# A post-LayerNorm attention and FFN block on one core: the order of the banded mix within a group of tokens

## What is computed

```python
# x: (4, 512, 1024); w1, w2: (1024, 1024)
attn = jnp.einsum('ds,td->st', w1, w2) * sparse_mask      # three stripes: a band beside the diagonal
y = jnp.einsum('bds,st->bdt', x, attn) + b2
x = _layernorm(x + gelu(y, approximate=False))
# w_l: dense (1024, 1024) weights, decoded from 4 bit planes and a 16-entry table per row
y = einsum('bsi,oi->bso', x, w_l) + bias                  # 8-bit weights where a row's norm is over 64
x = _layernorm(x + y)
```

## Time and profile before

| what | before |
|---|---|
| median of three runs | 306.03 us |
| the profiled execution | 305.57 us |
| its span | 303.8 us |
| PE busy | 289.7 us (95%) |
| DVE busy | 197.4 us (65%) |
| ACT busy | 184.7 us (61%) |
| POOL busy | 112.8 us (37%) |
| mean granted TensorE clock | 0.989 |

### The profile page before, as it was taken

How to read it: one execution, slowest core, us unless ns; L and a number is a source line. 1 busy time by engine, 2 the same in 40 slices (tenths; PEclk the granted TensorE clock), 3 DMA queues, 4 the chain that set the end, 5 groups by cost and what they waited for, 6 DMA issues and landing times.

```text
span 303.8 us, 5068 instructions
## 1 busy us (share of the span) xinstructions
PE 289.7 (95%) x1907; PEld 254.7 (84%) x1907; DVE 197.4 (65%) x352; ACT 184.7 (61%) x245; POOL 112.8 (37%) x178
## 2 busy tenths in 40 slices
PE   8999898999999999999999999999999999999980
PEld 4788766666769999999999999999998887888880
DVE  2679988997868977898776786504135445344362
ACT  1966558988998967976986979251144452312210
POOL 4000003343344988898788600000033333322321
PEclk9999999999999999999999999999999999999995
DMA  6999999999999301111110111119237785443222
GB/s 225 398 355 356 378 383 288 252 262 224 206 190 199 89 19 37 35 37 35 37 41 32 52 55 35 54 36 245 103 131 257 239 272 203 169 167 140 105 120 97
DMA packets 28480, 49.77 MB, mean 164 GB/s; under 512 B 2464, under 2 KB 11936, under 8 KB 28448
## 3 DMA queue, kind: packets, MB, share of 16 engines
q1 hardware_dynamic: 23392, 40.53, 39.1%
q0 software_dynamic: 4352, 8.39, 15.4%
q10 hardware_dynamic: 704, 0.46, 0.5%
HBM read 36.79 MB, written 12.58 MB: 163 GB/s over the span
## 4 chain that ended last, share of the span: by engine, by line
PE 80%; SPq 7%; DVE 4%; DMA 3%; ACT 2%; issue 2%; POOL 0%; DVEq 0%; ACTq 0%
PE acc L560 20%; PE acc L562 20%; PE acc L561 20%; PE acc L543 5%; PE acc L489 4%; DMA w<-in_w2d 3%; PE acc L464 2%; SPq L275 2%; PE acc L499 2%; PE acc L465 2%; PE acc L466 2%; SPq L279 1%; SPq L274 1%; PE acc L431 1%; PE acc L476 1%
## 5 line engine op out<-in xcount | busy, mean ns | idle before, releaser
L560 PE MATMUL acc<-lin,zz 128*128 128x256 f32 (+2 forms) x424 | 130.2, 307 | 0.3 <-issue 0.3
L562 PE MATMUL acc<-lin,zz 128*128 128x256 f32 (+2 forms) x424 | 129.8, 306 | 0.0
L561 PE MATMUL acc<-lin,zz 128*128 128x256 f32 (+2 forms) x424 | 129.6, 306 | 0.0
L560 PEld LDWEIGHTS acc<-lin,zz 128*128 128x128 f32 x424 | 80.0, 189 | 4.6 <-issue 0.5
L561 PEld LDWEIGHTS acc<-lin,zz 128*128 128x128 f32 x424 | 80.2, 189 | 4.0
L562 PEld LDWEIGHTS acc<-lin,zz 128*128 128x128 f32 x424 | 80.1, 189 | 4.1
L725 ACT ACTIVATE leaf<-planes,lut,flip 128x1024 f32<-128x1024 uint8 x56 | 67.4, 1238 | 1.3 <-DVE dest L999 1.3
L999 DVE COPY_PREDICATED leaf<-planes,leaf 128x1024 f32<-128x1024 uint8 x32 | 43.6, 1362 | 12.6 <-ACT leaf L725 11.8
L1394 POOL DMA_DIRECT2D z<-in_xr x16 | 19.5, 1220 | 70.9 <-ACT z L707 69.4
L828 ACT ACTIVATE junk<-rows,cols 128x1024 bf16<-128x1024 f32 x15 | 17.2, 1150 | 39.6 <-POOL cols L1368 39.6
L1366 POOL TENSOR_TENSOR cols<-cols 128x1 f32<-128x1 f32 x15 | 9.0, 603 | 74.6 <-DVE rows L1119 74.6
(11 more groups left out here) (110 smaller groups left out, 438.3 us busy)
## 6 DMA issues: line engine op xcount, KB each, us to landing
z<-in_xt SPq DMA_DIRECT2D x16, 512.0 KB, 9.4
z<-in_xr POOLq DMA_DIRECT2D x16, 512.0 KB, 8.7
out_rows<-rows SPq DMA_DIRECT2D x15, 512.0 KB, 2.9
out_rows<-parts SPq DMA_DIRECT2D x32, 128.0 KB, 1.7
rows<-out_rows SPq DMA_DIRECT2D x16, 256.0 KB, 2.7
w<-in_w1d SPq DMA_DIRECT2D x7, 512.0 KB, 9.2
off_band<-in_mask_rest SPq DMA_DIRECT2D x8, 448.0 KB, 4.4
w<-in_w2d SPq DMA_DIRECT2D x3, 584.0 KB, 9.0
```

The lines of the kernel that those rows point to most:

```text
L560: nc.tensor.matmul(bank, hi, w_hi, start=k == 0, stop=False)
L561: nc.tensor.matmul(bank, hi, w_lo, start=False, stop=False)
L562: last = nc.tensor.matmul(bank, lo, w_hi, start=False, stop=k == KB - 1)
```

## The change

In each group, TensorE now takes own products of units 0 to 3, then pairs 2, 0 and 1 with excess 0 between pair 2 and pair 0, then own products of units 4 to 7, then excess 1, pairs 5 and 3, excess 2, and pairs 4 and 6. Before, it was own 0 to 3, excess 0, pairs 0, 2; own 4 to 6, excess 1, pairs 1, 3, 5; own 7, excess 2, pairs 4, 6. ScalarE's and VectorE's lists follow the new order in which units are finished, and `MIX_STEPS` deals one decode step of group 0 and one of group 1 differently. The count of instructions of every kind in the mix is the same.

```diff
-    MIX_STEPS = [(3, 3), (2, 1), (2, 1), (2, 0)]
+    MIX_STEPS = [(3, 2), (3, 1), (2, 1), (2, 0)]
...
-    BESIDE = (0, 2, 1, 3, 5, 4, 6)
+    BESIDE = (2, 0, 1, 5, 3, 4, 6)
...
+                beside(g, 2)
                 excess(g, 0)
                 beside(g, 0)
-                beside(g, 2)
-                for t in (4, 5, 6):
+                beside(g, 1)
+                for t in (4, 5, 6, 7):
                     own(g, t)
-                excess(g, 1)
-                beside(g, 1)
-                beside(g, 3)
-                beside(g, 5)
-                own(g, 7)
                 if g == FIRST_TURN_GROUP:
                     pe.wait_ge(consts_made, 4)
                     turn(0)
+                excess(g, 1)
+                beside(g, 5)
+                beside(g, 3)
                 excess(g, 2)
                 beside(g, 4)
                 beside(g, 6)
...
                 gelu(g, 0)
-                done = decode_steps(MIX_STEPS[g][0], done)
+                if g == FIRST_TURN_GROUP:
+                    done = decode_steps(MIX_STEPS[g][0], done)
+                gelu(g, 1)
+                gelu(g, 2)
+                if g != FIRST_TURN_GROUP:
+                    done = decode_steps(MIX_STEPS[g][0], done)
+                for pair in MIX_Z.get(g, ()):
+                    make_z_hi(*pair)
+                if g == FIRST_TURN_GROUP:
+                    make_lin_hi(0)
                 if g + 1 < GROUPS:
                     make_xe_hi(g + 1)
-                gelu(g, 1)
-                if g + 1 < GROUPS:
                     make_x_hi(g + 1, 1)
-                if g == FIRST_TURN_GROUP:
-                    make_lin_hi(0)
-                gelu(g, 2)
-                gelu(g, 3)
-                for pair in MIX_Z.get(g, ()):
-                    make_z_hi(*pair)
-                done = decode_steps(MIX_STEPS[g][1], done)
-                gelu(g, 4)
-                gelu(g, 5)
+                for t in (3, 4, 5):
+                    gelu(g, t)
                 if g + 1 < GROUPS:
                     make_x_hi(g + 1, 3)
                 gelu(g, 6)
                 if g + 1 == GROUPS:
                     make_lin_hi(1)
                 gelu(g, 7)
+                done = decode_steps(MIX_STEPS[g][1], done)
...
-                done = decode_steps(MIX_STEPS[g][0], done)
+                if g == FIRST_TURN_GROUP:
+                    done = decode_steps(MIX_STEPS[g][0], done)
                 if g + 1 < GROUPS:
-                    make_xe_lo(g + 1)
                     make_x_lo(g + 1, 0)
-                    make_x_lo(g + 1, 1)
+                if g != FIRST_TURN_GROUP:
+                    done = decode_steps(MIX_STEPS[g][0], done)
                 for pair in MIX_Z.get(g, ()):
                     make_z_lo(*pair)
                 if g == FIRST_TURN_GROUP:
                     make_lin_lo(0)
-                if g != GROUPS - 2:
-                    done = decode_steps(MIX_STEPS[g][1], done)
                 if g + 1 < GROUPS:
+                    make_x_lo(g + 1, 1)
+                    make_xe_lo(g + 1)
                     make_x_lo(g + 1, 2)
                     make_x_lo(g + 1, 3)
                 else:
                     make_lin_lo(1)
-                if g == GROUPS - 2:
-                    done = decode_steps(MIX_STEPS[g][1], done)
+                done = decode_steps(MIX_STEPS[g][1], done)
```

## The result

| what | before | after |
|---|---|---|
| median of 22 runs each | 305.81 us | 306.56 us |
| ratio, after to before | | 1.0022, 95% interval 1.0014 to 1.0029 |
| the profiled execution | 305.57 us | 306.93 us |
| its span | 303.8 us | 305.1 us |

The change makes the kernel slower by 0.22%, some 0.7 us. The forecast was 306.1 us, 0.1 us over the 306.03 us that were known of the kernel before. Four of the 22 executions of after took 310.7 to 312.6 us, none of before did; the ratio leaves them out, and the last experiment shows in a trace what such an execution can be.

What follows compares the result with a forecast made beforehand. The mix was taken to end at a gate that ScalarE and VectorE open, so PE's gains are given back: -0.02 us by the walk, +0.1 for hand-overs, on the median 306.1 us; range 305.3 to 307.1.

Steps and rivals of the forecast that it cites:

- likeliest case: Whole kernel: the forecast of 306.1 us, with its own range from 305.5 to 306.6 us; chance 0.61.
- slower: Whole kernel: a time over 306.6 us, slower by more than 0.2%; chance 0.24.
- Rival B: PE's waits for itself cost more than a hand-over from another engine: 0.9 us more, 307.0 us; chance 0.20.
- Part 1, mode changes: PE in each group: four array mode changes instead of six, at 0.21 us each, save 0.42 us.
- Part 2, PE's waits for itself: Per group, pair 1 waiting for pair 0 adds 0.35 us, pair 4 waiting for pair 3 adds 0.12 us.
- Part 3, group 0: turn(0) waits some 1.6 us for gelu 1, starting at 47.62; group 1 starts at 52.25, before 52.48.
- Part 4: Groups 1 and 2: 12.30 us per group against 12.25 without a stall; group 1's old 0.6 us wait goes.
- Part 5, ScalarE's chain and the gate: Group 3: new 0.76 us stall for x_lo at own product 2; linear product at 93.69 us, before 93.71.
- Covers: Group 0's excess 0 loses its 0.47 us xe wait without gain; loads of x and xe have many microseconds of slack.
- A: PE's waits for itself cost nothing in the mix: 1.1 us less, 305.0 us; chance 0.15.
- C: Clock falls to 1.2 GHz in the new wait ahead of turn(0) in group 0: 310.5 us; chance 0.04.

Runs made afterwards that it cites:

- the last experiment: Changed kernel with gelu 1 of group 0 ahead of the third leaf and one group 3 leaf behind the last gelu: 305.49 to 312.09 us, traced execution 310.96 us.
- the first experiment: Changed kernel plus one needless wait per group, pair 3 also waiting for pair 5 right ahead of it: 307.68 us, ratio to before 1.0064.

## Why the prediction was right, and where it was not

The range held, and the likeliest case by a hair: 306.56 us, in 305.3 to 307.1, with "slower" from 306.6 on. Some of this is luck. The forecast was a change of 0.1 us on a base of 306.03; the change is 0.7 us, and the base, by 22 runs, 305.81. So the number was better than the reasoning, and what was missing is the mechanism of Rival B. By its own parts:

- **Part 1, mode changes.** The changed kernel shows them at the same size: 52.65 (the last of pair 6) to 52.97 and 0.34 to the next. The 0.42 us per group were saved: 12.25 - 0.42 and 0.68 of the waits below make 12.51, and a group took 12.55.
- **Part 2, PE's waits for itself: the step that failed.** Both terms were put too low, 0.35 for 0.45 us and 0.12 for 0.23. Pair 1 comes 0.57 us behind pair 0's last matmul (42.30 to 42.87) and 0.34 more to the next: 0.45 over two spacings of 0.23, where I had 0.35. Pair 4: 0.35 and 0.34, so 0.23, where I had 0.12. The modelled end was a good end (42.30 + 0.39 = 42.69); it was the hand-over from there that is 0.18 and not the 0.10 that I had carried over from VectorE to PE. In groups 1 and 2 this is 2 x 0.21 = 0.42 of the 0.51 us that were missing. A group has 0.68 us of such waits against 0.42 of mode changes saved: the exchange loses. The one more wait of the first experiment, 0.4 us per group, says the same.
- **Part 3, group 0.** turn(0) started 1.95 us behind the third leaf, predicted 1.92, behind a wait of 1.44 from the modelled end, 1.59 as the predicted 1.6 was counted. From the turn to group 1 it took 4.74 and not 4.63, pair 4's wait again. What I didn't ask is whether gelu 1 had to stand behind the leaf: the trace of before shows ScalarE idle for 0.63 us ahead of it, about the length of a gelu, and moving it there gained 1.5 us, twice what the whole change had lost.
- **Part 4.** The stall of 0.6 us in group 1 went, as forecast; the groups took 12.56 and 12.55 instead of 12.30, for the reason above.
- **Part 5, ScalarE's chain and the gate.** The stall at own product 2 of group 3 was there. The profile's 0.44 us are counted from the modelled end; counted as the 0.76 were, from the moment at which PE could have started (78.89 + 0.69 = 79.58) to 80.18, it is 0.60, since PE came later. From group 3 to the linear product 16.83 us passed, predicted 16.84, and this is in part luck: 2.10 us to own product 2 where 2.25 were predicted, and 14.73 from there where it was 14.59. The gate is L1020: 93.58 + 1.23 + 0.10 = 94.91. But "PE gets there sooner and waits, as it did before" says too little: taking a leaf out of the list gained nothing, so PE's pairs are as late as the list.
- **Covers.** "The loads have many microseconds of slack" was wrong for xe of group 3, and was so before the change: 0.24 us there, nothing now, since it lands, by 67.07 + 10.1, at the moment at which ScalarE wants it. In the profiled execution that cost nothing, so the sum was not hurt; it caps what can be won by a shorter PE stream, and it is the source of the one long execution that was traced.
- **The rivals.** A (the waits are free) is out by the rows of 0.18. B (they cost more) was right in its mechanism: by 0.10 and 0.11 per wait, just under the 0.12 from which I let it decide. C: the clock stayed at 1.00 over the wait ahead of turn(0):

```profile
46.00:50.00 4.00, 2.56 (x18) 1.00 0.93 345
50.00:60.00 10.00, 9.82 (x63) 1.00 0.84 153
```

It did fall once, in another kernel and behind 4.3 us.

## What to carry to other kernels

TensorE's wait for its own work of a moment ago is not free, even if nothing else is late: here 0.45 us if the partner stands right ahead and 0.23 with one matmul between, together more than the two mode changes that they were traded for (0.42). Taking such waits out again brings little while another engine's list stands right behind them. When a step is moved behind a gap in an engine's list, ask which short step could fill that gap, and who waits for it. And of each load list what frees its buffer: a load that is released by a moved step moves too. Its slack is what lies between its landing and its first reader, and has to be read there (here 0.24 us), not assumed.

## What the runs showed that I had not expected

- PE's hand-over to itself is 0.18 us from the modelled end of the last matmul, longer than the 0.10 from VectorE to PE (51.16 + 1.22 to 52.48); all eight waits of the first experiment are of that size.
- A load of 256 KB took 10.1 us with GpSimd's 512 KB loads beside it, 7.4 in the kernel that issued it ahead of them (65.38), and 13.9 in one execution of another.
- Behind 4.3 us of standing still PE ran at 1.2 GHz for at least 3.2 us and came back to full speed; behind 1.44 us it stayed at full speed.
